# Loads of the next batch issued ahead of the peaks, and one subtraction given from GpSimd to VectorE

## The chip, the cores and the metric

One core of a Trainium2 chip runs the whole kernel. The time is the device time of one launch in microseconds (us), as the median of three timed runs. One more execution was profiled; its records are what the rows below show. The engines are named PE (TensorE), PEld (its weight loads), DVE (VectorE), ACT (ScalarE), POOL (GpSimd) and SP (SyncE, which only issues transfers here; its queue is SPq).

## What is computed

A transformer block on 32 sequences of 256 tokens with 128 features. The attention has 16 heads of 8 features. To the usual logits it adds an incidence of two lines per head, weighted by a decay to the power of the distance; behind it stand a gated residual and a top-2 mixture of 8 experts:

```python
logits = einsum('bhqd,bhkd->bhqk', q, k) * scale
write_lines = exterior(x_prev @ w1_write.T, x @ w2_write.T)     # six numbers per token and head
read_lines  = exterior(x @ w1_read.T, x @ w2_read.T)
incidence = einsum('bqhp,bkhp->bhqk', read_lines, write_lines @ J6)
bias = incidence * decays ** (q - k) * (q > k) * bias_scale
attn = softmax(where(q < k, -inf, logits + bias))
x = x + ga * (attn @ v @ w_out.T + b_out)
x = x + gb * sum over the two best experts of weight * FFN_e(layernorm(x) * (1 + cb) + sb)
```

## The kernel before

It has a setup, the attention part (`attend`, all that the change touches) and the experts' part. The attention part works batch by batch, one sequence of 256 tokens at a time, in iterations b = -4 to 35. Each iteration has eight slots, p = 0 to 7, one for each pair of heads, and each engine has its own list of work, written out slot by slot; an engine takes its list strictly in order and waits on semaphores in it. The lists are pipelined over batches: in iteration b the scores, exponentials and values of batch b are made, the prescores of batch b + 1 (from slot 1 on), the projections and lines of batches b + 2 and b + 3, and the end of batches b - 1 to b - 3.

Matrix products run in bf16. To keep the precision, each fp32 number is split in three bf16 parts: the high part (ACT copies, L1179), the rest (POOL subtracts, L1259), the middle part (ACT, L1182) and the low part (POOL subtracts once more, L1264, 96x768). The parts of the q and k features are `dim_part`, those of the lines `line_part`. Their place in the products is along the partitions, so they take a way through DRAM. SP stores `dim_part` to `dim_rows` (`store_dims`) and `line_part` to `line_rows` (`store_lines`), six transfers each (L649), and loads them from there:

- `load_rows` (L676, L677): rows of eight heads (a half) into `KT` and `QF` (`queries` in the rows): the dims' part from `dim_rows` and the decayed lines' part from `line_rows`, two transfers each. The prescores wait for these: half 0 in slot 1 of the iteration before, half 1 in slot 5.
- `load_lines` (L686): undecayed lines into `KI` and `QI`, for the incidences.
- `load_peaks` (L691): the prescores give each query's maximum (its peak), which DVE reduces (L919, L924), POOL splits in three parts, PE turns (jobs max0 and max1) and ACT copies to `peakT`; SP then loads it into three more rows of `QF`. The scores of the first slot wait for the peaks of half 0, those of the fifth slot (p = 4) for half 1.

SP's list is its `body`: it is in order too, so a transfer behind a wait comes no sooner than the wait's end. The waits are `hold(...)`: for `used["max0"]` and `used["max1"]` (the peaks are in `peakT`), `line_low` and `dim_low` (the low parts are made), `lines_stored` and `dims_stored` (stores have landed), `sc_ready`, `pre_ready` and `inc_ready` (the target's last readers are done).

On PE the names are `pre` (prescores, L759 to L761), `sc` (incidences L732, scores L745 to L748) and `bank` (the jobs). On DVE `weigh` multiplies `sc` by the decay (L950). On POOL `decayed` (L1367) opens an iteration, `outer_products` (L589, four products of 128x256) and `crosses` (L601, L603) make the lines of batch b + 3, `line_values` scales them, and L1360 scatters tokens to the experts.

## Time and profile before

| | us |
|---|---|
| median of three timed runs | 1115.75 |
| lowest, highest | 1115.15, 1118.87 |
| the profiled execution | 1110.27 |
| its span, first to last instruction | 1108.5 |
| busy in the span: PE, POOL, DVE, ACT | 921.3, 813.4, 788.8, 710.5 |

The profile has one row for a group of instructions or for one moment on one engine. In a row of a timeline the first number is the start in us from the span's start, the second how long it took, then the engine, the line of the kernel, the operation, what is written and read (names without their numbers), and the shapes. Brackets at the end give idle time of the engine just before it, and what ended it. "issue" there means that no cause shows. PE's matmuls overlap, so their times are not to be added.

### The profile page before, as it was taken

Reading aid. Unit: us, or ns where it says so; the run is one execution under the profiler, and the core shown is the slowest. Engines: PE = TensorE matmul, PEld = TensorE weight load, DVE = VectorE, ACT = ScalarE, POOL = GpSimd, SP = SyncE. Lnnn points to the kernel's source line nnn. Section 1 sums busy time; section 2 is a strip of 40 time slices with the busy share of each in tenths; the row PEclk is TensorE's granted clock in tenths of the full one; section 3 lists DMA queues with packets and bytes.
Section 4 is the critical chain, followed back from the end, with each engine's and each line's share of the span. In section 5 each row is a group of like instructions: output and inputs, shape, how many; then the busy total and the mean of one; then the engine's idle time right before and its main releaser. Section 6 shows DMA issues by size and latency. Waiting matters only on the chain. (4 is left out here: it accounts for less than half of the span.)

```text
span 1108.5 us, 30436 instructions
## 1 busy us (share of the span) xinstructions
PE 921.3 (83%) x9281; PEld 722.1 (65%) x9281; DVE 788.8 (71%) x2095; ACT 710.5 (64%) x1580; POOL 813.4 (73%) x1352
## 2 busy tenths in 40 slices
PE   2437989989988898898988888988862899999966
PEld 2325667767676666676766666766641788888852
DVE  7576768776788788787788878778756455566536
ACT  2345778777787777787777877777562455555520
POOL 8355678887888888888888888888345366666644
PEclk9999999998999999999999999999895899999989
DMA  7345565554565656656566565665411353333339
GB/s 189 114 127 150 160 163 145 155 160 139 153 173 148 176 148 161 168 144 179 145 165 164 151 176 141 161 167 152 119 50 48 84 167 88 95 92 92 86 140 349
DMA packets 233853, 160.37 MB, mean 145 GB/s; under 512 B 57376, under 2 KB 220512, under 8 KB 233568
## 3 DMA queue, kind: packets, MB, share of 16 engines
q1 hardware_dynamic: 222416, 133.77, 45.4%
q0 software_dynamic: 8448, 17.45, 5.1%
q10 hardware_dynamic: 2832, 7.20, 1.7%
q8 instruction: 81, 1.33, 0.6%
q14 instruction: 76, 0.62, 0.2%
HBM read 81.38 MB, written 76.19 MB: 142 GB/s over the span
## 5 line engine op out<-in xcount | busy, mean ns | idle before, releaser
L919 DVE TENSOR_REDUCE peak<-pre 128x6 f32<-128x768 f32 x256 | 244.2, 954 | 79.5 <-PE pre L761 76.5
L1152 ACT ACTIVATE PT<-sc 128x768 f32<-128x768 f32 x256 | 204.9, 800 | 31.0 <-PE sc L748 28.6
L950 DVE TENSOR_TENSOR sc<-sc,decay 128x512 f32<-128x512 f32 x256 | 177.2, 692 | 29.2 <-PE sc L732 25.5
L1638 POOL DMA_INDIRECT yab<-y_out,xt x136 | 131.6, 968 | 83.1 <-issue 63.3
L1360 POOL DMA_INDIRECT xg<-stage,slot_i x128 | 130.9, 1023 | 60.9 <-issue 31.2
L759 PE MATMUL pre<-KT,queries 84*128 84x128 bf16 x512 | 116.8, 228 | 58.6 <-DMA queries<-line_rows 52.3
L761 PE MATMUL pre<-causal,identb 128*128 128x256 bf16 x512 | 144.8, 283 | 0.0
L760 PE MATMUL pre<-KT,queries 84*128 84x256 bf16 x512 | 143.7, 281 | 0.0
L1592 DVE TENSOR_TENSOR hid<-silu,up 128x256 f32<-128x256 f32 x136 | 57.3, 421 | 82.6 <-ACT silu L1546 82.6
L745 PE MATMUL sc<-queries,KT 87*128 87x128 bf16 x512 | 101.8, 223 | 14.7 <-issue 3.6
L759 PEld LDWEIGHTS pre<-KT,queries 84*128 84x128 bf16 x512 | 51.2, 100 | 92.7 <-DMA queries<-line_rows 60.5
L1546 ACT ACTIVATE silu<-up 128x256 f32<-128x256 f32 x136 | 52.4, 385 | 88.9 <-PE up L1482 88.9
L732 PE MATMUL sc<-QI,KI 100*128 100x128 bf16 x1024 | 101.6, 222 | 0.0
L748 PE MATMUL sc<-queries,KT 87*128 87x128 bf16 x512 | 101.1, 222 | 0.0
L747 PE MATMUL sc<-queries,KT 87*128 87x128 bf16 x512 | 101.0, 222 | 0.0
L589 POOL TENSOR_TENSOR outer<-lines 128x256 f32<-128x256 f32 x116 | 80.7, 728 | 6.0 <-ACT lines L1117 6.0
L1498 PE MATMUL y<-w,hidT 128*128 x544 | 83.1, 275 | 0.1
L775 PE MATMUL pv<-PT,VP 128*32 128x256 f32 x1024 | 82.2, 393 | 0.0
L745 PEld LDWEIGHTS sc<-queries,KT 87*128 87x128 bf16 x512 | 50.9, 99 | 37.5 <-issue 25.9
L1498 PEld LDWEIGHTS y<-w,hidT 128*128 128x128 f32 x544 | 71.4, 191 | 0.3 <-issue 0.3
L732 PEld LDWEIGHTS sc<-QI,KI 100*128 100x128 bf16 x1024 | 70.3, 99 | 0.1
L1480 PE MATMUL up<-queries,x_hi 128*128 x136 | 66.0, 485 | 0.0
(275 smaller groups left out, 2672.1 us busy)
## 6 DMA issues: line engine op xcount, KB each, us to landing
line_rows<-line_part SPq DMA_DIRECT2D x64, 216.0 KB
dim_rows<-dim_part SPq DMA_DIRECT2D x64, 192.0 KB, 2.1
KT<-dim_rows SPq DMA_DIRECT2D x64, 192.0 KB
queries<-dim_rows SPq DMA_DIRECT2D x64, 192.0 KB
line_rows<-line_part SPq DMA_DIRECT2D x64, 144.0 KB
KI<-line_rows SPq DMA_DIRECT2D x64, 144.0 KB
QI<-line_rows SPq DMA_DIRECT2D x64, 144.0 KB
xt<-xg SPq DMA_DIRECT2D x136, 65.0 KB, 1.9
```

What stands on the lines that cost most here:

```text
L732: last = nc.tensor.matmul(seeded(p)[:, n, t, :], KI[0:INC, h, blk], QI[0:INC, h, blk], start=n == 0 and t == 0, stop=True, skip_group_chec ...
L745: nc.tensor.matmul(seeded(p)[:, n, 0, :], KT[par][0:TOP, h, first], QF[par][0:TOP, h, first], start=False, stop=True, skip_group_check=True)
L748: last = nc.tensor.matmul(seeded(p)[:, n, 1, :], KT[par][0:TOP, h, second], QF[par][0:TOP, h, second], start=False, stop=True, skip_group_ ...
L759: nc.tensor.matmul(pre[:, n, 0:P], QF[par][0:DIMS + LINES, h, 0:P], KT[par][0:DIMS + LINES, h, 0:P], start=True, stop=False)
L760: nc.tensor.matmul(pre[:, n, P:3 * P], QF[par][0:DIMS + LINES, h, P:T], KT[par][0:DIMS + LINES, h, :], start=False, stop=False)
L761: last = nc.tensor.matmul(diagonal(pre, n), identb[:], causal[:].unsqueeze(1).broadcast_to([P, 2, P]), start=False, stop=True)
L919: nc.vector.reduce_max(peak[half][:, i:i + 2, 0:3], pre[:, :, 0:3 * P].rearrange("p n (g k) -> p n g k", g=3), AX.X)\
L950: nc.vector.tensor_tensor(seeded(p), seeded(p), decay[:, 2 * p:2 * p + 2, :].unsqueeze(2).broadcast_to([P, 2, NT, P]), ALU.mult).then_inc( ...
L1152: nc.scalar.activation(PT[p % 4][:], sc[:, window], ACT.Exp).then_inc(exped.sem, 1)
L1360: nc.gpsimd.indirect_dma_start(xg[0:E * CAP, :], bass.IndirectOffsetOnAxis(slot_i[:, t, k:k + 1], 0), stage[par][:, t, k, :], None).then_i ...
L1498: last = nc.tensor.matmul(y[r % 2][:, 0:D], hidT[r % 2][:, m * P:(m + 1) * P], w3[:, span(e, 1), m, :].rearrange("p e d -> p (e d)"), star ...
L1638: nc.gpsimd.indirect_dma_start(yab, bass.IndirectOffsetOnAxis(xt[r][:, D:D + 1].bitcast(i32), 0), y_out[r % 8][:], None).then_inc(y_sent[r ...
```

## The change

`load_rows` is cut in two: `load_dims` loads the dims' part and `load_decayed` the lines' part. For half 1 both now stand at the head of SP's iteration, in front of the wait for the peaks of half 1. For half 0 the dims' part stands right behind the line stores, in front of the wait for the peaks of half 0, and the decayed part behind these peaks, in front of the lines of half 1. The low part of the lines (L1264) is taken from POOL's slot 3 and given to DVE's slot 3, behind that slot's reduce of the prescores.

```diff
-                def load_rows(jb, par, half):
+                def load_dims(jb, par, half):

                     hold(dims_stored, jb)
-                    hold(lines_stored, jb)
                     hold(sc_ready, jb - 2, 4 * half + 4)
                     hold(pre_ready, jb - 1, 4 * half + 1)
...
+                        sp.dma_start(tile[0:DIMS, heads, :], dim_rows[jb % 3][kq, :, heads, :]).then_inc(rows_loaded[half].sem, 16)
+
+                def load_decayed(jb, par, half):
+
+                    hold(lines_stored, jb)
+                    hold(sc_ready, jb - 2, 4 * half + 4)
...
+                        sp.dma_start(tile[DIMS:PEAK0, heads, kq * P:kq * P + P], line_rows[jb % 3][kq, :, heads, T:LW])\
+                          .then_inc(rows_loaded[half].sem, 16)
...
                 def body(b, par):
+                    if live(b + 1):
+                        load_dims(b + 1, 1 - par, 1)
+                        load_decayed(b + 1, 1 - par, 1)
                     if live(b):
                         load_peaks(b, par, 1)
                     if live(b + 1):
-                        load_rows(b + 1, 1 - par, 1)
                         load_lines(b + 1, 0)
                     if live(b + 2):
                         store_lines(b + 2)
+                        load_dims(b + 2, par, 0)
                     if live(b + 1):
                         load_peaks(b + 1, 1 - par, 0)
+                    if live(b + 2):
+                        load_decayed(b + 2, par, 0)
+                    if live(b + 1):
                         load_lines(b + 1, 1)
-                    if live(b + 2):
-                        load_rows(b + 2, par, 0)
                     if live(b + 3):
                         store_dims(b + 3)
```

The subtraction:

```diff
+                    if p == 3 and live(b + 2):
+                        wait(dve, line_mid, b + 2)
+                        nc.vector.tensor_tensor(line_part[:, 2, :], line_rest[:], line_part[:, 1, :], ALU.subtract).then_inc(line_low.sem, 1)
...
-                        if p == 3 and live(b + 2):
-                            wait(pool, line_mid, b + 2)
-                            nc.gpsimd.tensor_tensor(line_part[:, 2, :], line_rest[:], line_part[:, 1, :], ALU.subtract).then_inc(line_low.sem, 1)
```

How the lists stand in one iteration. SP before, from the peaks of half 0 (first row) over the lines and the rows to the six stores of the dims:

```order
98 L691 DMA queries<-peakT 3x8x256
99 L686 DMA KI<-line_rows 36x8x256
100 L686 DMA QI<-line_rows 36x8x256
101 L676 DMA KT<-dim_rows 48x2048
102 L677 DMA KT<-line_rows 36x8x128
103 L676 DMA queries<-dim_rows 48x2048
104 L677 DMA queries<-line_rows 36x8x128
105 L649 DMA dim_rows<-dim_part 128x3x256
```

SP now, from the end of the line stores to the first store of the dims:

```order
97 L649 DMA line_rows<-line_part 96x384
98 L675 DMA KT<-dim_rows 48x2048
99 L675 DMA queries<-dim_rows 48x2048
100 L697 DMA queries<-peakT 3x8x256
101 L683 DMA KT<-line_rows 36x8x128
102 L683 DMA queries<-line_rows 36x8x128
103 L692 DMA KI<-line_rows 36x8x256
104 L692 DMA QI<-line_rows 36x8x256
105 L649 DMA dim_rows<-dim_part 128x3x256
```

The dims' loads moved in front of the peaks, and the decayed loads in front of the lines. Next comes the head of the following iteration. SP before, from the last store of the dims:

```order
110 L649 DMA dim_rows<-dim_part 128x256
111 L691 DMA queries<-peakT 3x8x256
112 L676 DMA KT<-dim_rows 48x2048
113 L677 DMA KT<-line_rows 36x8x128
114 L676 DMA queries<-dim_rows 48x2048
115 L677 DMA queries<-line_rows 36x8x128
116 L686 DMA KI<-line_rows 36x8x256
```

SP now, at the same place:

```order
110 L649 DMA dim_rows<-dim_part 128x256
111 L675 DMA KT<-dim_rows 48x2048
112 L675 DMA queries<-dim_rows 48x2048
113 L683 DMA KT<-line_rows 36x8x128
114 L683 DMA queries<-line_rows 36x8x128
115 L697 DMA queries<-peakT 3x8x256
116 L692 DMA KI<-line_rows 36x8x256
```

All four loads of half 1 now stand between the stores and the peaks of half 1. POOL before, from the rest (L1259) to the counts of the experts:

```order
474 L1259 TENSOR_TENSOR line_rest<-line_val,line_part 96x768
475 L589 TENSOR_TENSOR outer<-lines 128x256 x4
476 L1264 TENSOR_TENSOR line_part<-line_rest,line_part 96x768
477 L601 TENSOR_TENSOR cross<-outer 128x2x2x48
478 L603 TENSOR_TENSOR cross<-outer 128x4x16 x3
```

DVE now, around its fourth slot, where L929 is the reduce of the prescores and L960 the multiply by the decay:

```order
595 L960 TENSOR_TENSOR sc<-sc,decay 128x512
596 L929 TENSOR_REDUCE peak<-pre 128x2x3
597 L991 TENSOR_TENSOR line_part<-line_rest,line_part 96x768
598 L1017 TENSOR_REDUCE slot_i<-slot_pick 128x4
599 L1021 TENSOR_SCALAR eg<-egap 128x2
600 L1023 RECIPROCAL stage<-eg 128x2
601 L1026 TENSOR_SCALAR stage<-egap,stage 128x1 x2
602 L960 TENSOR_TENSOR sc<-sc,decay 128x512
```

The row L1264 is gone from POOL, so `crosses` follows `outer` directly, and it is L991 on DVE.

## Rows read from the trace of the kernel before

**Rows 1.** Stretches: us, busy of PE, PEld, DVE, ACT, POOL, clock, DMA, GB/s

```profile
93.90:203.80 109.90, 98.48 (x1162) 75.84 (x1162) 80.68 (x171) 82.30 (x157) 82.07 (x154) 1.00 0.58 156
203.80:302.80 99.00, 88.06 (x983) 69.28 (x982) 71.50 (x178) 71.94 (x144) 81.74 (x150) 0.91 0.54 149
302.80:762.60 459.80, 410.96 (x4901) 317.68 (x4900) 372.83 (x881) 361.29 (x720) 402.64 (x740) 0.99 0.60 160
762.60:821.60 59.00, 49.20 (x612) 36.95 (x612) 43.41 (x115) 35.59 (x64) 26.57 (x58) 0.94 0.44 114
234.50:237.90 3.40, 3.40 (x19) 3.34 (x18) 1.22 (x2) 0.60 (x1) 2.12 (x4) 0.50 0.22 64
```

**Rows 2.** Timeline of POOL over one regular batch

```profile
397.80 0.72 POOL L1367 TENSOR_TENSOR line_val<-line_val,line_decay 96x256 f32<-96x256 f32 x1
...
399.13 0.20 POOL L1331 CAST peak_part<-peak_rest 128x16 bf16<-128x16 f32 x1 [0.17 <-POOL peak_rest L1328]
...
402.90 2.78 POOL L589 TENSOR_TENSOR outer<-lines 128x256 f32<-128x256 f32 x4
405.64 1.66 POOL L1264 TENSOR_TENSOR line_part<-line_rest,line_part 96x768 bf16<-96x768 f32 x1
407.25 0.60 POOL L601 TENSOR_TENSOR cross<-outer 128x192 f32<-128x192 f32 x1
...
419.65 1.16 POOL L1293 TENSOR_TENSOR dim_part<-dim_rest,dim_part 128x512 bf16<-128x512 f32 x1
420.76 0.73 POOL L1367 TENSOR_TENSOR line_val<-line_val,line_decay 96x256 f32<-96x256 f32 x1
```

**Rows 3.** Timeline of PE: scores of the fifth slot, prescores of the second

```profile
405.75 0.22 PE L745 MATMUL sc<-queries,KT 87*128 87x128 bf16 x1 [0.23 <-issue]
...
421.56 0.23 PE L759 MATMUL pre<-KT,queries 84*128 84x128 bf16 x1 [1.38 <-DMA queries<-line_rows]
```

**Rows 4.** Timeline of SP in the same batch

```profile
402.62 0.76 SPq L691 DMA_DIRECT2D queries<-peakT  x1
...
407.90 2.89 SPq L649 DMA_DIRECT2D line_rows<-line_part  x6
414.14 0.74 SPq L691 DMA_DIRECT2D queries<-peakT  x1
...
416.16 0.32 SPq L676 DMA_DIRECT2D KT<-dim_rows  x1
...
420.91 3.04 SPq L649 DMA_DIRECT2D dim_rows<-dim_part  x6
```

**Rows 5.** Waits of PE, first and last stretch: total us, times, longest

```profile
PE pre L759 <- DMA queries<-line_rows: 9.4, 9, 1.9
...
PE pre L759 <- DMA queries<-line_rows: 4.2, 2, 2.3
```

**Rows 6.** Timeline of PE before a stretch at half clock

```profile
233.92 0.23 PE L759 MATMUL pre<-KT,queries 84*128 84x128 bf16 x1 [2.35 <-DMA queries<-line_rows]
```

**Rows 7.** DVE with two inputs from SBUF, and POOL beside it

```profile
L589 DVE TENSOR_TENSOR outer<-lines 128x256 f32<-128x256 f32 x12 | 4.3, 421 | 10.5 <-ACT lines L1117 10.5
...
419.84 1.03 DVE L970 TENSOR_TENSOR hot<-iota,topi 128x32 f32<-128x32 f32 x1
...
1098.78 0.68 DVE L1624 TENSOR_TENSOR ya<-ya,x_all 128x512 f32<-128x512 f32 x1
...
1098.95 1.64 POOL L1645 TENSOR_TENSOR ya<-ya,x_all 128x512 f32<-128x512 f32 x1 [0.46 <-DVE ya L1617]
```

**Rows 8.** Timeline of DVE around the subtraction's new place

```profile
403.90 0.96 DVE L919 TENSOR_REDUCE peak<-pre 128x6 f32<-128x768 f32 x1
...
406.51 0.70 DVE L950 TENSOR_TENSOR sc<-sc,decay 128x512 f32<-128x512 f32 x1 [0.23 <-PE sc L732]
407.96 0.96 DVE L919 TENSOR_REDUCE peak<-pre 128x6 f32<-128x768 f32 x1 [0.75 <-PE pre L761]
```

**Rows 9.** Timeline of ACT at the middle part of the lines

```profile
402.97 0.84 ACT L1182 ACTIVATE line_part<-line_rest 96x768 bf16<-96x768 f32 x1 [0.44 <-POOL line_rest L1259]
```

More of the change, by code:

```diff
@@ L666, in store_lines @@
                         spread(slots(line_rows[jb % 3][kq]), line_part[:, :, kq * LW:(kq + 1) * LW], kq, lines_stored.sem)
-                def load_rows(jb, par, half):
+                def load_dims(jb, par, half):
                     hold(dims_stored, jb)
+                    hold(sc_ready, jb - 2, 4 * half + 4)
+                    hold(pre_ready, jb - 1, 4 * half + 1)
+                    heads = slice(8 * half, 8 * half + 8)
+                    for kq, tile in ((0, KT[par]), (1, QF[par])):
+                        sp.dma_start(tile[0:DIMS, heads, :], dim_rows[jb % 3][kq, :, heads, :]).then_inc(rows_loaded[half].sem, 16)
+                def load_decayed(jb, par, half):
                     hold(lines_stored, jb)
                     hold(sc_ready, jb - 2, 4 * half + 4)
-                    hold(pre_ready, jb - 1, 4 * half + 1)
-                    heads, done = slice(8 * half, 8 * half + 8), rows_loaded[half].sem
+                    heads = slice(8 * half, 8 * half + 8)
                     for kq, tile in ((0, KT[par]), (1, QF[par])):
-                        sp.dma_start(tile[0:DIMS, heads, :], dim_rows[jb % 3][kq, :, heads, :]).then_inc(done, 16)
-                        sp.dma_start(tile[DIMS:DIMS + LINES, heads, kq * P:kq * P + P],
-                                     line_rows[jb % 3][kq, :, heads, T:LW]).then_inc(done, 16)
+                        sp.dma_start(tile[DIMS:PEAK0, heads, kq * P:kq * P + P], line_rows[jb % 3][kq, :, heads, T:LW])\
+                          .then_inc(rows_loaded[half].sem, 16)
                 def load_lines(jb, half):
```

## Prediction

> **What bounds the kernel now.** I started with the stretches of the span [rows 1]. The attention part, 94 to 822 us, is the only part that the change touches. Between 302.80 and 762.60, 20 batches take 459.80 us, 22.99 each. PE is busy 410.96 us of that and POOL 402.64, so the shares do not say which of them is the limit. The order of time does. On POOL [rows 2] the decay multiply (L1367) opens one batch at 397.80 and the next at 420.76: 22.96 us. Read the starts and ends of the rows between: each begins where the one before ends, and where the row carries a wait it is a wait for POOL's own result (0.17 us). POOL is a chain with no slack, and most batches of this stretch repeat its 22.96 to within 0.03. So here the batch lasts as long as POOL's list of work.
>
> PE meanwhile has one halt per batch that it would not have by its own work [rows 3]: the prescores of the second slot start at 421.56 after 1.38 us of waiting for the rows of half 0. SP shows why [rows 4]: the peaks of half 0 are issued at 414.14, then the lines, and only at 416.16 the rows, which land 5.4 us later, at 421.56. Without the halt PE would need 22.96 - 1.38 = 21.58 us a batch. POOL is the longer of the two, so in the regular stretch the halt is idle time of an engine that is not the limit.
>
> It is the limit elsewhere. In the first stretch, 93.90 to 203.80, the rows cost PE 9.4 us in nine halts, and in the last, from 762.60, 4.2 us in two [rows 5]; POOL is busy only 82.07 of 109.90 us and 26.57 of 59.00 us there [rows 1]. Between 203.80 and 302.80 four batches take 24.75 us each and the granted clock is 0.91. The halt that ends at 233.92 lasted 2.35 us [rows 6], and from 234.50 to 237.90 the clock is 0.50, the 1.2 GHz level [rows 1]. I read it so: a long halt of PE comes first, then a stretch at half clock, and that one delays the next rows again.
>
> **The change part by part.** *The last subtraction leaves POOL.* L1264 starts at 405.64 and the next row at 407.25 [rows 2]: 1.61 us off POOL's chain. What stands behind it is `crosses`, which waits for `outer`, POOL's own result. Until now 1.61 us of other work lay between them. A wait for an own result costs 0.17 us where it shows in [rows 2], and nothing at all if the result is ready; I take 0.12 back.
>
> *It comes to VectorE.* The trace has no 96x768 subtraction on VectorE. Two inputs from SBUF at 256 columns take 0.42 us (L589, alone), at 512 columns 0.68 (L1624) [rows 7]: 0.26 more for 256 more, so 0.94 us for 768. Its place is behind the reduce that starts at 403.90 and ends at 404.86 [rows 8]. Its input is there: ACT's middle part runs 402.97 to 403.81 [rows 9]. VectorE has 0.75 us of waiting for PE in front of the reduce at 407.96 [rows 8], plus 0.23 in front of the multiply at 406.51; 0.98 us covers 0.94. What is over (waiting for a port, below) delays the multiply by some 0.3 to 0.7 us, and its reader, the scores of the sixth slot, has PE's own prescores in front of it. So I cost VectorE at nothing in the regular stretch.
>
> *But it holds POOL up.* This is where I chose. In the last part of the kernel POOL adds 128x512 from SBUF while VectorE does an addition with both inputs in SBUF: VectorE's runs from 1098.78 to 1099.46, POOL's starts at 1098.95 and takes 1.64 us [rows 7]. POOL's own subtraction of 128x512 takes 1.16 (419.65) [rows 2]; the 0.48 more is just the time to VectorE's end. It goes the other way too: L970, a comparison of 128x32, takes 1.03 us and ends at 420.87, 0.06 after POOL's subtraction ends at 420.81 [rows 7, 2]. The new subtraction would start at 404.86, while POOL is in its four `outer` products (402.90 to 405.68) [rows 2]. It waits out the product that runs, up to 0.7 us (2.78 / 4), and then holds the next for its own 0.94. Bounds: 0 (the products don't mind) and 0.94; I take 0.94, because the rows show both directions.
>
> The Trainium skill (SBUF — State Buffer, SBUF: two separate sides) says that VectorE with two SBUF inputs and a GpSimd instruction that reads SBUF share one pair of ports, and that whoever is second is blocked for the whole instruction; the trace agrees (0.48 and 1.03 us). It speaks against this change. The same skill (GPSIMD Engine Reference, Engine selection) sends elementwise work to VectorE as about twice as fast, which by itself would make the move worth its full 1.61 us, 30 us in this stretch instead of 11.
>
> POOL's chain is then 22.96 - 1.61 + 0.12 + 0.94 = 22.41 us, still above PE's 21.58. The 20 batches gain 20 x 0.55 = **11.0 us**.
>
> *Rows of half 1 in front of the peaks of half 1.* They were issued behind the peaks (402.62). Now they follow the six stores of the dims, which end at 420.91 + 3.04 = 423.95 [rows 4], so they are out by about 426, and need to be there by the prescores of the sixth slot, some 6 us later. These halts go. The price is on the peaks, which now stand behind four big loads (rivals).
>
> *Rows of half 0.* The dims' part goes in front of the peaks' wait, right behind the line stores. These end at 407.90 + 2.89 = 410.79 today; on SP nothing happens until 414.14, so this part is free. With VectorE's result at about 405.9 in place of 407.30 the stores themselves start up to 1.4 us earlier. The decayed part follows the peaks at about 415.2, ahead of the lines. PE is due at 421.56 - 1.38 = 420.18. With today's 5.4 us from the first issue to the last landing the decayed part is there at 420.6, 0.4 late; but it is two loads and not four, and the lines' loads stand behind it and not in front. So of the halt 0 to 0.4 us is left; I take 0.
>
> *What the halts give.* 203.80 to 302.80: without long halts the clock should stay up, and POOL's chain is next: 4 x (24.75 - 22.41) = 9.4 us; I take **8**, since one fall may stay. 93.90 to 203.80: of 9.4 us I take **5.5**, as the last batches there meet POOL's 22.41. From 762.60: **3.5** of 4.2.
>
> Sum: 11.0 + 8 + 5.5 + 3.5 = 28 us. The profiled execution took 1110.27 us (span 1108.5), so 1082.3. The median of the three timed runs is 1115.75, 5.5 above it; I carry the difference along: **1088 us**, 2.5% faster. Its own range is 1080 to 1095.
>
> **Rivals.**
> *POOL is not held.* Then its chain is 21.47 and PE's 21.58 is next: 20 x 1.38 = 27.6, 12.7 in the four batches, 7 and 4 outside: 51 us, 1065. For it: L589 on VectorE ran at 0.42 us in the prologue, which shows that nothing is lost when POOL is not reading at the time; a product of 0.7 us may leave gaps between its reads. Against: [rows 7].
> *The halt moves to the peaks of half 1.* They are issued behind the rows, which follow the stores of the dims: rows out from about 424.2, landing 4.6 to 5.4 us later (5.4 as above; the lower end is an estimate, since the lines are not in front), 428.8 to 429.6, and the peaks just behind. PE's scores of the fifth slot, at 405.75 now [rows 3], are due at 428.71: a wait of 0.1 to 0.9 us in the regular stretch. There it costs little, since PE has 22.41 - 21.58 = 0.83 us to spare, and it cannot be earlier by itself: the exponential in front of it stands behind ACT's middle part, which waits for POOL (0.44 us) [rows 9]. In the other stretches, where PE leads, it could eat most of the 17 us: 1115.75 - 11 - 3 = 1101 (1095 to 1107). The same result comes if the decayed rows of half 0 still come late.
> *Slower.* The same mechanism, larger. If the peaks land more than 0.83 us after PE is due, the batch is PE's: 21.58 + w. From w = 1.38 (landing about 1.4 us behind PE's own due time) it is longer than now. At w = 2, with the peaks behind six stores and four loads, it is 0.6 us a batch, 17 us over 28 batches, and halts of this size are those that the half clock followed: 3.4 us at 0.50 costs 1.7 us of PE. That gives 1133, and 1120 with few falls. Against it: the loads start as soon as dims are stored, and 28 batches would all have to lose.
> *No change.* POOL's hold grows to what was taken off (a wait for an own result of 0.17, a second product held) and the clock falls stay.
>
> **How the numbers follow.** Forecast 0.52 (1088); POOL not held 0.13 (1065); moved halt 0.20 (1101); no change 0.07; slower 0.08 (1133). Faster by over 0.3% (3.3 us, about what a measurement of this kernel can tell): 0.85; within: 0.07; slower: 0.08. The range leaves out the far half of the first rival and all of the last two: 1066 to 1107.
>
> **What the new profile would show.** Right: L1264's work on VectorE at 0.95 to 1.65 us, one `outer` product per batch at about 1.65 in place of 0.73, POOL without waits and a period of 22.4 us; the rows' waits in front of the prescores nearly gone; the clock near 1.00 between 204 and 303 us. POOL unheld: `outer` at 0.73 throughout and a period of 21.5. Moved halt: PE waits at the scores for `queries<-peakT`. Most likely to make me wrong is the hold: its size is from one pair of operations in another part of the kernel.

## The result, and the profile after

The changed kernel took **1104.05 us** (median of 4 runs, 1099.33 to 1107.09), beside 1117.31 us for the kernel before (median of 4, 1115.15 to 1121.72). The ratio is 0.9877, with a 95% interval of 0.9837 to 0.9918: 13 us or 1.2% faster. The forecast was 1088 us, a gain of 28. The sign held, and the time lies in the wide range of 1066 to 1107, but outside the forecast's own of 1080 to 1095. A little less than half of the gain came, and the time is near that of the rival "the halt moves to the peaks of half 1" (1101).

The profiled execution took 1104.48 us, its span 1102.7. That is 0.4 us above its own median, while the profiled execution of before lay 7 us below its median; so the two traces show only 5.8 us of the 13. The stretches of after run between the same places as those of [rows 1] (start of the scores of batches 0, 5, 9 and 29, end of the last scores). The columns are the stretch and its length, busy time of PE, PEld, DVE, ACT and POOL, the granted clock, DMA share and GB/s:

```profile
94.00:203.50 109.50, 99.91 (x1163) 76.47 (x1164) 86.20 (x176) 82.98 (x157) 78.69 (x150) 0.95 0.61 158
203.50:294.60 91.10, 81.88 (x982) 63.74 (x982) 77.28 (x181) 73.03 (x144) 77.56 (x145) 0.98 0.63 162
294.60:762.60 468.00, 415.50 (x4902) 322.00 (x4902) 383.08 (x902) 365.51 (x720) 385.22 (x721) 0.96 0.60 157
762.60:816.90 54.30, 46.25 (x612) 35.21 (x611) 43.44 (x117) 35.64 (x64) 24.15 (x56) 1.00 0.43 116
```

Against [rows 1] the first stretch gains 0.4 us (5.5 expected), the second 7.9 (8), the last 4.7 (3.5). The twenty regular batches, which were to gain 11.0, **lose 8.2**: 23.40 us each instead of 22.99. POOL's busy time there fell as meant, from 402.64 to 385.22 us. The clock fell too, from 0.99 to 0.96.

PE's waits over the whole span tell which thing came last now (total us, times, longest):

```profile
PE sc L755 <- DMA queries<-peakT: 57.3, 32, 3.9
...
PE pre L769 <- DMA queries<-line_rows: 2.5, 1, 2.5
```

L755 is the scores' first product (L745 before) and L769 the prescores' (L759 before). The rows' waits of [rows 5] and of the regular stretch ([rows 3]: 1.38 us) are gone but for one. In their place stand 57.3 us of waiting for peaks: one wait in every batch from 1 to 30 at the fifth slot, for the peaks of half 1, and two of 0.5 us for those of half 0.

How that comes about is seen in a bad batch, 452.8 to 479.4. POOL first, and the same list in time order for SP, ACT and PE:

```profile
455.20 1.16 POOL L1303 TENSOR_TENSOR dim_part<-dim_rest,dim_part 128x512 bf16<-128x512 f32 x1
...
472.73 0.20 POOL L1336 CAST peak_part<-peak 128x16 bf16<-128x16 f32 x1 [4.13 <-DVE peak L934]
```

```profile
456.45 3.52 SPq L649 DMA_DIRECT2D dim_rows<-dim_part  x6
460.23 0.99 SPq L675 DMA_DIRECT2D KT<-dim_rows  x1
461.27 0.42 SPq L675 DMA_DIRECT2D queries<-dim_rows  x1
461.87 0.31 SPq L683 DMA_DIRECT2D KT<-line_rows  x1
462.23 0.41 SPq L683 DMA_DIRECT2D queries<-line_rows  x1
462.76 0.74 SPq L697 DMA_DIRECT2D queries<-peakT  x1
```

```profile
460.27 0.37 ACT L1138 ACTIVATE peakT<-bank 24x256 bf16<-24x256 f32 x1 [0.18 <-PE bank L828]
```

```profile
467.48 0.27 PE L755 MATMUL sc<-queries,KT 87*128 87x128 bf16 x1 [3.85 <-DMA queries<-peakT]
```

ACT has the peaks ready at 460.64. SP issues their load at 462.76, 2.12 us later, since it has first to issue the six stores of the dims (from 456.45, right behind POOL's low part, 456.36) and four loads. (The loads need the dims stored one iteration earlier, so it is the order of SP's list that ties them to these stores, and not their landing.) From the issue to PE's start it is another 4.72 us. PE's late scores make its prescores late, DVE's maxima with them, and POOL then waits 4.13 us for DVE. POOL's low part of the next dims comes out of the same list, and the next peaks stand behind it. The change tied PE's fifth slot to POOL by way of SP, and so made a ring: POOL's dims, stores, loads of rows, load of peaks, scores, prescores, maxima, POOL.

A plain batch (203.5 to 225.7, 22.21 us) has the same order with less of it:

```profile
206.78 3.04 SPq L649 DMA_DIRECT2D dim_rows<-dim_part  x6
210.09 0.33 SPq L675 DMA_DIRECT2D KT<-dim_rows  x1
...
211.96 0.75 SPq L697 DMA_DIRECT2D queries<-peakT  x1
```

```profile
215.53 0.22 PE L755 MATMUL sc<-queries,KT 87*128 87x128 bf16 x1 [1.56 <-DMA queries<-peakT]
```

Of the 24 batches between 203.5 and 762.6, sixteen have a halt of 0.95 to 1.92 us there and eight one of 2.3 to 3.9. The batches with a halt of up to about 1.6 us and a full clock last 21.6 to 22.3, as if there were none. The eight last 24.0 to 26.6. The second thing that they have, most of them, is the clock. These are stretches of after again: the bad batch, one without a fall, and the fall in the bad one:

```profile
452.80:479.40 26.60, 22.37 (x246) 16.93 (x245) 18.82 (x46) 18.44 (x36) 19.60 (x37) 0.87 0.51 139
524.70:546.80 22.10, 20.05 (x246) 15.61 (x246) 19.33 (x46) 18.15 (x36) 19.23 (x37) 1.00 0.59 165
...
465.70:472.50 6.80, 5.02 (x37) 3.47 (x38) 1.80 (x4) 2.58 (x5) 2.14 (x6) 0.50 0.73 219
```

The halt starts at 463.63, the clock goes to 0.50 (1.2 GHz) at 465.7, within it, and is back at 472.5. PE is busy 2.3 us longer in that batch for the same 246 products.

The last part of the change that the trace shows is the hold of POOL. DVE's subtraction (L991) and POOL beside it, in another regular batch, and the group of the products on the page (busy us, mean ns of one):

```profile
394.95 1.42 DVE L991 TENSOR_TENSOR line_part<-line_rest,line_part 96x768 bf16<-96x768 f32 x1
```

```profile
393.47 3.49 POOL L589 TENSOR_TENSOR outer<-lines 128x256 f32<-128x256 f32 x4
397.03 0.59 POOL L601 TENSOR_TENSOR cross<-outer 128x192 f32<-128x192 f32 x1
```

```profile
L589 POOL TENSOR_TENSOR outer<-lines 128x256 f32<-128x256 f32 x116 | 99.9, 892 | 1.0 <-ACT lines L1130 1.0
```

The four products took 2.78 us [rows 2] and take 3.49 now: 0.71 more, all of it in one of the four (27 of the 116 products take 1.43 to 1.45 us, the others some 0.73).

### The profile page after: what moved, and what is told of

The parts are those of the page before. It is cut to its first block and busy times, and to the rows that moved or that the text cites. A ratio compares the mean times of both kernels' runs of the same rounds, so it can differ in the third digit from the quotient of the medians.

```text
span 1102.7 us, 30500 instructions
## 1 busy us (share of the span) xinstructions
PE 917.4 (83%) x9281; PEld 719.1 (65%) x9281; DVE 812.4 (74%) x2127; ACT 716.0 (65%) x1580; POOL 782.5 (71%) x1320
## 3 DMA queue, kind: packets, MB, share of 16 engines
q8 instruction: 81, 1.33, 0.5%
## 5 line engine op out<-in xcount | busy, mean ns | idle before, releaser
L929 DVE TENSOR_REDUCE peak<-pre 128x6 f32<-128x768 f32 x256 | 243.9, 953 | 56.5 <-PE pre L771 53.6
L960 DVE TENSOR_TENSOR sc<-sc,decay 128x512 f32<-128x512 f32 x256 | 177.0, 692 | 46.8 <-PE sc L742 41.4
L755 PE MATMUL sc<-queries,KT 87*128 87x128 bf16 x512 | 101.8, 224 | 64.9 <-DMA queries<-peakT 57.3
L769 PE MATMUL pre<-KT,queries 84*128 84x128 bf16 x512 | 116.9, 228 | 9.8 <-DVE peak L929 6.3
L1602 DVE TENSOR_TENSOR hid<-silu,up 128x256 f32<-128x256 f32 x136 | 57.3, 421 | 81.3 <-ACT silu L1556 81.3
L755 PEld LDWEIGHTS sc<-queries,KT 87*128 87x128 bf16 x512 | 51.4, 100 | 92.3 <-issue 76.7
L589 POOL TENSOR_TENSOR outer<-lines 128x256 f32<-128x256 f32 x116 | 99.9, 892 | 1.0 <-ACT lines L1130 1.0
L769 PEld LDWEIGHTS pre<-KT,queries 84*128 84x128 bf16 x512 | 51.5, 101 | 38.3 <-issue 15.3
```

The lines of the kernel that those rows point to most:

```text
L755: nc.tensor.matmul(seeded(p)[:, n, 0, :], KT[par][0:TOP, h, first], QF[par][0:TOP, h, first], start=False, stop=True, skip_group_check=True)
L769: nc.tensor.matmul(pre[:, n, 0:P], QF[par][0:DIMS + LINES, h, 0:P], KT[par][0:DIMS + LINES, h, 0:P], start=True, stop=False)
L929: nc.vector.reduce_max(peak[half][:, i:i + 2, 0:3], pre[:, :, 0:3 * P].rearrange("p n (g k) -> p n g k", g=3), AX.X)\
L960: nc.vector.tensor_tensor(seeded(p), seeded(p), decay[:, 2 * p:2 * p + 2, :].unsqueeze(2).broadcast_to([P, 2, NT, P]), ALU.mult).then_inc( ...
```

## The experiments

Each run is compared with runs of the kernel before on the same chip. "Middle" is the length of batches 5 to 28, from the trace, over 24. There is one trace for each kernel.

| kernel | median us | ratio to before (95%) | middle us per batch |
|---|---|---|---|
| before | 1115 to 1118 | 1 | 23.28 |
| after | 1104.05 | 0.9877 (0.9837 to 0.9918) | 23.30 |
| e1: after, rows of half 1 back | 1079.31 | 0.9681 (0.9635 to 0.9727) | 22.20 |
| e2: new order, subtraction on POOL | 1114.95 | 0.9998 (0.997 to 1.0026) | 23.39 |
| e3: before, subtraction on DVE | 1105.73 | 0.9902 (0.9858 to 0.9947) | 22.92 |
| e4: before, rows of half 0 moved | 1101.91 | 0.9857 (0.981 to 0.9904) | 22.96 |
| e5: after, peaks of half 1 on ACT's queue | 1081.23 | 0.9717 (0.9664 to 0.977) | 22.21 |
| e8: after, only the dims' rows in front | 1087.54 | 0.972 (0.967 to 0.977) | 22.82 |
| e6: e1, subtraction one slot later | 1132.33 | 1.0125 (1.0077 to 1.0173) | 23.84 |
| e9: e1, subtraction of 32 columns | 1062.09 | 0.9517 (0.9467 to 0.9566) | 21.52 |
| e10: e1, two steps of POOL on ACT | 1058.02 | 0.9477 (0.9426 to 0.9528) | 21.37 |

My theory after the result: the rows of half 1 in front of the peaks cost what is missing, by the ring above. The rivals: the subtraction on DVE does harm (by the hold, or by making DVE late), or the new order of half 0 does.

### e1: the rows of half 1 behind the peaks again

```diff
                 def body(b, par):
-                    if live(b + 1):
-                        load_dims(b + 1, 1 - par, 1)
-                        load_decayed(b + 1, 1 - par, 1)
                     if live(b):
                         load_peaks(b, par, 1)
                     if live(b + 1):
+                        load_dims(b + 1, 1 - par, 1)
+                        load_decayed(b + 1, 1 - par, 1)
                         load_lines(b + 1, 0)
```

> The changed kernel with one thing put back: the four row loads of half 1 stand behind the peaks of half 1 again. Half 0 in two parts and the subtraction on VectorE stay. Theory A (the peaks of half 1 land late because they stand behind the row loads of half 1): PE's 57 us of waiting for the peaks at the fifth slot go to near 0, the prescores' waits stay under 10 us, the regular batch takes what POOL's chain takes, 22.96 - 1.61 + 0.71 + 0.1 = 22.2 us, and the time is 25 to 32 us under the kernel before. Theory B (the peaks are late because the whole stream of transfers is too dense since the subtraction and half 0 came earlier): most of the 57 us stays, and the time is within 5 us of the changed kernel.

It took 1079.31 us (1077.91 to 1081.23), 3.2% under the kernel before (1116.12). That is theory A, with a larger gain than its 25 to 32 us (36.8). The stretch of batches 5 to 28, PE's waits (whole span) and POOL's (in that stretch) in this kernel:

```profile
203.30:736.20 532.90, 491.25 (x5882) 375.24 (x5881) 464.34 (x1082) 432.10 (x864) 463.04 (x865) 1.00 0.63 166
```

```profile
PE pre L768 <- DMA queries<-line_rows: 8.2, 10, 2.3
...
PE sc L754 <- DMA queries<-peakT: 4.9, 9, 0.9
```

```profile
POOL xg L1369 <- issue: 29.4, 84, 0.7
```

and POOL's in the same batches of after (203.5 to 762.6):

```profile
POOL peak_part L1336 <- DVE peak L934: 26.3, 19, 4.1
```

Two things follow. The 559.1 us of after are 26.2 more than the 532.9 here, and after's POOL waits 26.3 us for DVE's maxima, which here it does not wait for at all. The loss of the middle batches is the ring. And the waits for rows are 8.2 us in ten, not the 52.3 in 41 of before. All ten are of half 1, and the kernel before had such waits too. Two of before's, both at the sixth slot and so for half 1, then one of e1's:

```profile
109.42 0.23 PE L759 MATMUL pre<-KT,queries 84*128 84x128 bf16 x1 [1.04 <-DMA queries<-line_rows]
152.53 0.23 PE L759 MATMUL pre<-KT,queries 84*128 84x128 bf16 x1 [1.04 <-DMA queries<-line_rows]
```

```profile
109.88 0.23 PE L768 MATMUL pre<-KT,queries 84*128 84x128 bf16 x1 [1.47 <-DMA queries<-line_rows]
```

Sorted by slot, before's 9.4 us in the first stretch are 6.1 us of half 0 and 3.3 us of half 1; in batches 5 to 28 they are 35.0 us of half 0 and 1.6 us of half 1. So **in the middle batches the rows of half 1 had hardly ever been late**, and there the move of half 1 paid for nothing. In the first batches they had been, and were again in e1 (4.4 us from 94.1 to 203.3). The clock is 1.00 over the middle stretch of e1.

### e2 and e3: each part of the change by itself

e2 puts the subtraction back on POOL and keeps the new order.

```diff
-                    if p == 3 and live(b + 2):
-                        wait(dve, line_mid, b + 2)
-                        nc.vector.tensor_tensor(line_part[:, 2, :], line_rest[:], line_part[:, 1, :], ALU.subtract).then_inc(line_low.sem, 1)
...
+                        if p == 3 and live(b + 2):
+                            wait(pool, line_mid, b + 2)
+                            nc.gpsimd.tensor_tensor(line_part[:, 2, :], line_rest[:], line_part[:, 1, :], ALU.subtract).then_inc(line_low.sem, 1)
```

> The whole new order of SP, with the subtraction back on POOL. If POOL's chain is what binds the regular batch, as I read it, its period is again 22.96 us or more, and the wait for the peaks of half 1 shows here too (0.1 to 0.9 us a batch by the landing estimate). Time: 0 to 8 us under the kernel before. If POOL's list was no limit, this kernel is as fast as the changed one, 13 us under before.

1114.95 us (10 runs, 1109.96 to 1117.75), ratio 0.9998: the new order alone is worth nothing. Its waits for peaks are nearly those of after, and POOL's products are at their old length:

```profile
PE sc L755 <- DMA queries<-peakT: 51.9, 31, 3.6
```

```profile
L589 POOL TENSOR_TENSOR outer<-lines 128x256 f32<-128x256 f32 x116 | 80.7, 725 | 1.1 <-ACT lines L1127 1.1
```

So the halt at the peaks is not made by DVE's subtraction, and the hold is.

e3 is the kernel before with the subtraction on DVE and the old order; against the kernel before, its edit is the subtraction's part of the change and nothing else.

> The kernel before with the subtraction on VectorE and nothing else. POOL's chain is then 22.2 us, but PE's halt for the rows of half 0 stays in the loop. In stretches where POOL caught up before, the batch took 22.2 to 22.6 us with this halt. So the regular batch takes 22.3 to 22.8 us; gain 4 to 12 us. If the halt alone had bound the batch, the gain is 0; if POOL alone had, it is 15 us or more.

1105.73 us (10 runs, 1100.08 to 1115.6), 10 us faster. Here PE halts for the rows as before, 41.7 us in batches 5 to 28 (before: 36.5), and the clock in those batches is 0.97. It is less the halts than the clock that lengthens them: 9 of the 24 have a fall of the clock and last 23.8 to 26.0 us, the other 15 have halts of 1.2 to 2.6 us and a median length of 22.1. The kernel before has seven batches with a fall. The group of L601 in e3:

```profile
L601 POOL TENSOR_TENSOR cross<-outer 128x192 f32<-128x192 f32 x29 | 24.5, 845 | 2.3
```

POOL's four products are at 724 ns here, but this one is at 845 instead of 601 (and L603 at 385 instead of 326). So in e3 DVE's subtraction meets another instruction of POOL, or none.

### e4: the rows of half 0 moved, and nothing else

The diff to after is that of e1 and that of e2 together.

> The kernel before with the new order of half 0 alone: half 1 stays behind its peaks and the subtraction on POOL. PE's waits for the rows go to near 0 and so do the stretches at half clock; the regular batch stays at POOL's 22.96 us. The gain is what the other stretches give, 12 to 20 us. If the halts had been the limit in the regular batch too, the period falls below 22.9 and the gain comes near the 36 us of the kernel with the subtraction on VectorE.

1101.91 us (1099.49 to 1104.22) beside 1118.13. Nearly all the rows' waits are gone, with half 1 in its old place; nine of the ten left are of half 1:

```profile
PE pre L768 <- DMA queries<-line_rows: 6.9, 10, 2.3
...
PE sc L754 <- DMA queries<-peakT: 2.3, 5, 0.7
```

The middle batches last 22.96 us, as POOL's chain in [rows 2], and the clock over them is 1.00, with one fall in 24 batches. That is the prediction's reading of what bounds the kernel, seen from the other side: with the halts of half 0 gone and POOL's list untouched, the batches at full clock do not get shorter, and the 7.8 us that the middle gains are those of the batches with a fall.

These four and the two whole kernels make a table of parts. The subtraction alone gives 10 us, half 0 alone 16, both 37 (e1): each takes away what limits the other. By the ratios, half 1 costs some 16 us on top of e4 (e2: 0.9998 against 0.9857) and some 22 on top of e1 (after: 0.9877 against 0.9681).

### e5: the peaks of half 1 loaded from ACT's queue

What in the order makes the halt: that the peaks' load is issued late, or that it travels behind the rows? In e5 the order of SP is that of after, but ACT issues the load of these peaks itself, right behind its copy.

```diff
-                    if live(b):
-                        load_peaks(b, par, 1)
...
                                 evacuate(name, jb, jb % 2)
+                                if name == "max1":
+                                    wait(act, used["max1"], jb)
+                                    act.dma_start(QF[jb % 2][PEAK0:TOP, 8:16, :], peakT[1][:]).then_inc(peak_loaded[1].sem, 16)
```

> The changed kernel with the peaks of half 1 loaded from ACT's own DMA queue, right behind ACT's copy, in place of SP's. The row loads of half 1 stay at the head of SP's iteration. If the peaks were late because they stood in SP's list and in SP's queue behind the rows, they land about 2.3 us after issue and the 57 us of waits go below 10; the time is 22 to 32 us under before, less up to 0.8 us a batch that the issue may cost ACT. If the 16 DMA engines' bandwidth is what makes them late, they land 3.4 us or more after issue and at least half of the waits stays.

1081.23 us (1079.43 to 1086.13), 35 us under before and nearly as e1. ACT's copy, its load, and PE's start in one batch, and PE's waits over the span:

```profile
211.59 0.37 ACT L1136 ACTIVATE peakT<-bank 24x256 bf16<-24x256 f32 x1 [0.18 <-PE bank L826]
212.00 0.74 ACTq L1189 DMA_DIRECT2D queries<-peakT  x1
```

```profile
215.64 0.22 PE L753 MATMUL sc<-queries,KT 87*128 87x128 bf16 x1 [0.69 <-DMA queries<-peakT]
```

```profile
PE sc L753 <- DMA queries<-peakT: 23.5, 24, 2.0
```

The load is out 0.04 us after the copy, and it is still 3.64 us until PE starts. In after's plain batch it was 3.57. Over all middle batches in which PE waited for these peaks, the time from issue to PE's start is 3.64 to 4.45 us in e5 (median 3.90) and 2.39 to 4.72 in after (median 3.65). In the kernel before, where a load of peaks with no rows just ahead of it is seen to release PE, it is issued at 781.92 and PE starts at 784.29, 2.37 us. And in e10 below, where the same peaks go out 0.5 to 2.0 us behind the six stores but in front of the rows, PE starts 2.83 us after the issue without any wait in 22 of 24 middle batches, so they had landed by then. So both of the expectation's cases are half true. With the rows' loads beside it the small load mostly takes some 1.2 us longer, **whichever queue it is in** (in this batch of e5 two of the four loads go out just before it and two just after); and on SP's queue it is issued later besides, 1.33 us after the copy (median of the middle batches in after). One pause stays unexplained: in e1 PE stands still for 0.62 us at this place in nearly every batch, up to 3.51 us after the issue, and the profile names no cause. For the time only the later issue matters. In the middle batches, 16 waits of up to 1.5 us, 14.9 in all, leave them at 22.21 us, as 5 waits for peaks and 2.7 us do in e1. POOL, which sets those, does not wait for DVE's maxima here. In these kernels a halt of PE below some 1.6 us is free; it is the longer ones that turn the ring.

### e8: only the dims' rows in front of the peaks

```diff
                     if live(b + 1):
                         load_dims(b + 1, 1 - par, 1)
-                        load_decayed(b + 1, 1 - par, 1)
                     if live(b):
                         load_peaks(b, par, 1)
                     if live(b + 1):
+                        load_decayed(b + 1, 1 - par, 1)
```

> The changed kernel with only two of the four row loads of half 1 (the dims' part, 384 of 528 KB) in front of its peaks, the decayed part behind them. If the peaks wait for what stands in front of them, they are issued 0.8 us earlier and land up to 0.7 us sooner after issue: PE's 57 us of waiting falls to 15 to 35, and the time is between the changed kernel and the one with nothing in front, 20 to 30 us under before. If the kind of load in front makes no difference, it stays at the changed kernel's 13 us.

1087.54 us (1082.29 to 1090.13). Two loads in front of the peaks instead of four, and between the two ends: PE waits 27.5 us for peaks (22 times, longest 2.4). The loads of peaks do not land sooner after their issue than in after (median 3.61 us until PE starts, against 3.65, where the expectation had up to 0.7 less); they are issued sooner, 0.43 us after the copy (median) and not 1.33. POOL's wait for the maxima in batches 5 to 28 is

```profile
POOL peak_part L1336 <- DVE peak L934: 14.9, 10, 2.6
```

The stretch (199.4 to 747.0) is 547.6 us long, 14.7 more than e1's: again the length of that one wait. What PE waits in total does not give the price; POOL's wait does.

e8 also shows what moving half 1 can buy. Its first stretch takes 105.3 us (94.1 to 199.4), where the kernel before takes 109.9 and e1 109.2: the rows' halts of half 1 are gone there, and no halt at the peaks has come in their place.

### e6: the subtraction one slot later

The hold comes from DVE's subtraction falling on POOL's products. In the next slot POOL scatters, and the products are over; so I moved it there, from e1.

```diff
-                    if p == 3 and live(b + 2):
+                    if p == 4 and live(b + 2):
```

> The fastest kernel so far (half 1 behind its peaks, half 0 in two parts, subtraction on VectorE) with VectorE's subtraction one slot later, in its fifth. There POOL has its wait of 0.7 us and a scatter. If the hold needs a POOL instruction that reads SBUF, all four outer products take 0.73 us again and POOL's chain is 21.5 us. But the line stores start some 3 us later, and the decayed rows and the peaks of half 0 stand behind them: either PE waits for those up to 1 us a batch. Between 15 us faster than that kernel (only the hold counts) and 10 us slower (only the late stores count); I expect 5 slower.

1132.33 us (1128.47 to 1136.53), 1.25% **slower** than before, and by the ratios 4.6% slower than e1, for one digit. That is about 50 us, where I expected 5. The products are free (DVE 0.94 us, POOL's products 726 ns), but the hold is not all gone: DVE's subtraction now overlaps a short copy of POOL's, 0.20 us alone:

```profile
298.55 0.63 POOL L1335 CAST peak_part<-peak 128x16 bf16<-128x16 f32 x1
```

The larger loss is elsewhere. The line stores wait for this subtraction. SP, ACT and PE at the next first slot, and POOL's wait in batches 5 to 28:

```profile
415.49 2.86 SPq L649 DMA_DIRECT2D line_rows<-line_part  x6
418.61 0.31 SPq L675 DMA_DIRECT2D KT<-dim_rows  x1
418.97 0.42 SPq L675 DMA_DIRECT2D queries<-dim_rows  x1
419.80 0.73 SPq L697 DMA_DIRECT2D queries<-peakT  x1
```

```profile
419.33 0.37 ACT L1137 ACTIVATE peakT<-bank 24x256 bf16<-24x256 f32 x1 [0.17 <-PE bank L827]
```

```profile
423.52 0.22 PE L754 MATMUL sc<-queries,KT 87*128 87x128 bf16 x1 [1.29 <-DMA queries<-peakT]
```

```profile
POOL peak_part L1335 <- DVE peak L933: 37.0, 25, 4.2
...
POOL dim_part L1302 <- ACT dim_part L1220: 10.3, 5, 2.4
```

The peaks of half 0 are issued 0.10 us after their copy, so nothing stands in their way on SP; but the six stores and the two loads of dims have just gone out, and PE starts 3.72 us after the issue. It is the effect of e5, at the other half: what is in flight counts, not only what is in front in SP's list. The account of the middle batches needs more than the wait for the maxima this time: against e9 below, which has no hold, they are 55.7 us longer, 37.0 for the maxima, 10.3 for ACT's middle part of the dims, and 8.4 in which POOL is busy, which is about what that copy takes longer.

### e9: what the hold is worth

e9 is e1 with DVE's subtraction on 32 of the 768 columns. The low parts of the other columns are left out; a memset before the batches, not shown, makes them zero.

```diff
-                        nc.vector.tensor_tensor(line_part[:, 2, :], line_rest[:], line_part[:, 1, :], ALU.subtract).then_inc(line_low.sem, 1)
+                        nc.vector.tensor_tensor(line_part[:, 2, 0:32], line_rest[:, 0:32], line_part[:, 1, 0:32], ALU.subtract).then_inc(line_low.sem, 1)
```

> The fastest kernel so far with VectorE's subtraction on 32 of the 768 columns; the low part of the other columns is left out (zero). VectorE's instruction falls from 0.95 us to about 0.2, so nothing of POOL is held for longer than 0.1 us. If the hold and POOL's chain bound the batch, its period falls from 22.2 to 21.5 or 21.6 us (21.58 is PE's own), and 12 to 17 us of time go. If PE or ACT bind already, it stays at 22.2 and the time within 3 us.

1062.09 us (1061.03 to 1063.51), 4.8% under the kernel before where e1 is 3.2% under it. The instruction itself, still at the same place (duration ns, least, median and most), and its neighbour on POOL:

```profile
L990 DVE TENSOR_TENSOR line_part<-line_rest,line_part x32: 178/660/675, 59.8 to 729.4; 96x32 bf16<-96x32 f32 x32
```

```profile
L589 POOL TENSOR_TENSOR outer<-lines 128x256 f32<-128x256 f32 x116 | 80.7, 727 | 1.1 <-ACT lines L1130 1.1
```

The instruction takes 0.18 us alone and 0.66 beside POOL: it waits 0.48 us for a product of POOL to end, which with 0.95 + 0.48 is also the 1.42 of the full one. Its own 0.18 us hold nobody. The middle batch is 21.52 us, 0.68 under e1's 22.20, close to the 0.71 of the hold, and POOL's chain is still what the batch follows.

### e10: two small steps of POOL on ACT

If POOL's chain is the limit in e1, anything taken off it counts, where ACT has room (432.10 of 532.90 us busy). The two 128x2 steps of the second norm (L1321, L1322 in after) go to ACT's first slot. Nothing of the computation is left out.

```diff
+                        if p == 0 and live(b - 2):
+                            wait(act, var2, b - 2)
+                            wait(act, shift2, b - 3)
+                            nc.scalar.activation(ve2[:], mv2[:, :, 1], ACT.Copy, bias=EPS).then_inc(norm_step2.sem, 1)
+                            nc.scalar.activation(nm2[:], mv2[:, :, 0], ACT.Copy, scale=-1.0).then_inc(norm_step2.sem, 1)
...
-                    wait(pool, var, jb)
-                    settle(pool, pool_settled)
-                    nc.gpsimd.tensor_scalar(ve[:], mv[:, :, 1], EPS, None, ALU.add).then_inc(stepped.sem, 1)
-                    nc.gpsimd.tensor_scalar(nm[:], mv[:, :, 0], -1.0, None, ALU.mult).then_inc(stepped.sem, 1)
```

> The fastest kernel so far with two more short instructions taken from POOL: the two steps of the second norm (128x2, 0.31 us each from start to start) are done by ACT in the slot before. POOL's chain is 22.2 - 0.6 = 21.6 us; ACT, busy 18 us a batch, gets 0.5 us more. If POOL's list binds the batch: 12 to 15 us faster than that kernel, 48 to 52 us under before. If ACT's new work delays the exponentials, or PE binds: within 4 us of it.

**1058.02 us** (1055.62 to 1059.71), 5.2% under the kernel before (1115.14), 57 us where I expected 48 to 52, and the fastest of all; it beats both kernels of this study. The middle batch went from 22.20 to 21.37, 0.83 us, for 0.62 us of instructions. POOL and DVE in one batch:

```profile
404.26 2.79 POOL L589 TENSOR_TENSOR outer<-lines 128x256 f32<-128x256 f32 x4
407.13 1.20 POOL L601 TENSOR_TENSOR cross<-outer 128x192 f32<-128x192 f32 x1
```

```profile
406.51 1.36 DVE L990 TENSOR_TENSOR line_part<-line_rest,line_part 96x768 bf16<-96x768 f32 x1
```

The hold has moved: POOL is ahead by those 0.6 us, its products end in peace, and DVE's subtraction now falls on L601, which takes 1.20 us instead of 0.60. It waits 0.41 us for the last product, runs its own 0.95 and ends at 407.87; POOL's instruction ends 0.46 later. The hold is 0.6 instead of 0.71, which is part of the 0.83. PE's waits for rows are up again (16.7 us, 16 times), all of them for half 1: as the batch gets shorter, the old place of half 1 begins to be late in the middle batches too (8.3 us there). PE is close behind POOL by now.

## Why the prediction was right, and where it failed

**What bounds the kernel: right.** POOL's list sets the regular batch; e4 (22.96 with PE's halts gone) and e9 and e10 (each shortening of POOL arrives at the end) show it. The reading of the rows was a little too clean. Between the rows of [rows 2] POOL has other pauses than those for its own results, in front of its four scatters:

```profile
409.80 1.10 POOL L1360 DMA_INDIRECT xg<-stage,slot_i  x1 [0.69 <-DVE peak L924]
```

Over the 24 middle batches they add up to nearly the same in before, after, e1, e6, e9 and e10 (32.7 to 33.8 us), so I count them as part of the list's length.

**POOL's chain: right.** It was to be 22.96 - 1.61 + 0.12 + 0.94 = 22.41 us. In e1, where nothing else stands in the way, it is 22.20. The hold was the term chosen between 0 and 0.94; it measured 0.71, so its mechanism was right and its size 0.23 us too large. The rest, 0.14, agrees with the 0.12 for the own result. The place was right too: one of the four products. The rival "POOL is not held" gets its number from e9: without the hold it would have been 0.7 us a batch more, some 16 us over the middle batches.

By the Trainium skill (SBUF — State Buffer, SBUF: two separate sides) whoever of the two comes second at the shared pair of ports is blocked for the whole instruction of the other. The traces agree but for 0.14 us: POOL's product in after ends 0.59 us after DVE's subtraction where alone it takes 0.73, and e10's L601 ends 0.46 after it where alone it takes 0.60. With a start just behind DVE's, that is why the hold is 0.71 and not 0.95. The Trainium skill (GPSIMD Engine Reference, Engine selection) sends elementwise work to VectorE as about twice as fast as GpSimd. Here it is 0.95 us against 1.65, and the 0.71 of the hold comes back from it.

**The rows of half 0: right.** I left nothing of the halt, and in after, e1 and e4 no prescores of batches 5 to 28 wait for rows of half 0 (35.0 us before). The 1.9 and 1.4 us of such waits that e1 and e4 have there are of half 1.

**DVE at no cost: right.** DVE's work is 1.42 us, within 0.95 to 1.65, and in e1, which has it too, the middle batches' waits for DVE add up to 0.2 us at PE and 2.9 at POOL.

**203.8 to 302.8: right** (8 forecast, 7.9 in after, 10.0 in e1). **The first stretch: wrong**, of 5.5 us came 0.4 in after and 0.7 in e1. The traces show what stood there: in after, where the rows' halts are gone, 4.8 us of waiting for the peaks and one fall of the clock (192.6), in e1 4.4 us of rows of half 1 and one fall (132.1). e8 has neither, no fall and 105.3 us, a gain of 4.6. So the term had a right size and came out only where neither half was late. The stretch varies between kernels up to 119.1 us (e6), and with one trace each I can't say how much of that is chance.

**The rows of half 1: here the prediction failed**, in three steps. In its sum the peaks that wait behind these rows cost nothing; by the traces of after and e1 they cost some 23 us.

*Little was bought.* I wrote "These halts go" of half 1, and no row stood behind it. [rows 3] shows a halt at half 0, [rows 5] adds up the line without saying which half. Of the 52.3 us before, 46.0 are of half 0; half 1 has 1.6 us in the middle batches and 3.3 in the first stretch. e4, with half 1 in its old place, has 6.9 us left over the whole span. A look at which slot the waits are in would have said so.

*The price was mis-sized.* I put the wait for the peaks at 0.1 to 0.9 us, from a landing at 428.8 to 429.6. It was 0.95 to 3.94 in the regular batches, 1.8 on average over the 32 waits. In a plain batch the landing was nearly right: from the end of the six stores to PE's start it is 5.71 us (209.82 to 215.53), which from the forecast's 423.95 gives 429.7. Against the 428.71 at which PE was to be due that is a wait of 0.95, and it was 1.56. So most of the error there is PE: I took its own batch as 21.58, the period less the halt. But some of PE's other waits of the batch before were slack as well; in e10 the middle batches last 21.37 on average and the shortest 20.84. So PE arrives earlier than I thought and waits longer, and, for the same reason, can afford more: not 0.83 us but some 1.6.

*"It costs little" was true of most batches and not of eight.* In those the halt was 2.3 to 3.9 us, POOL had to wait for PE's maxima, and most were followed by a stretch at half clock. Their share is what turned a gain into a loss in the middle: the eight halts are some 12 us over 1.6 each, and nine batches with a fall of the clock have PE busy 1.3 to 2.7 us longer. The sum, an estimate of some 27 us, is close to the 26.2 that e1 does not have. The "slower" rival had this mechanism (ring and clock) and its threshold of w about 1.4; I thought that "28 batches would all have to lose", but eight were enough to take back what sixteen gained.

What stays open is why it was those eight. In all of them the peaks were issued late, 1.64 to 2.80 us after ACT's copy (most of the others: about 1 us), and PE started 3.2 to 4.7 us after the issue; four others had an issue 1.5 to 2.2 us late too, but there PE started 2.4 to 2.8 us after it. In five of the eight the six stores took 3.5 to 4.9 us to issue instead of 3.04 (3.52 in the bad batch above), in the other three the loads of rows came more slowly. Why SP was slower just there no run was made to tell.

With e1's number the forecast reads as follows: the parts that were argued from rows give 29.0 us in the profiled executions (1110.27 to 1081.23), for 28 forecast, and the one part that had no row took about 23 back. That the 29.0 meets the 28 is in part luck. The profiled execution of before is a fast one, and by the medians e1 gains 36.8 us. And by stretches e1 gains 0.7, 10.0, 15.9 and 1.9 us, where 5.5, 8, 11.0 and 3.5 were forecast: the errors of the first and the third cancel.

## What to carry to other kernels

A transfer in front of another in a queue is a price on the one behind, even when SP has time: look first whether the one moved forward had ever been waited for, by slot and not by line. A small load that an engine waits for should go out before the big ones whose readers come later. And where an engine has spare time per batch, a halt costs nothing up to that, and beyond it everything: price halts by the wait that they cause at the engine that sets the period (here POOL's for the maxima, 0, 14.9 and 26.3 us in e1, e8 and after, against 0, 14.7 and 26.2 us of time). That price is of one wait only: in e6, with 37.0 us of it, other waits and a hold come to another 19 us against e9.

## What the runs showed of the hardware

- The load of `peakT` (24x256) took 2.37 us from issue to the start of its reader with no loads of rows just ahead, 3.57 behind four of them on the same queue (2.39 to 4.72 over the middle batches, median 3.65), and 3.64 on another engine's queue with two of the four just ahead and two just behind (3.64 to 4.45, median 3.90). Another queue gave an earlier issue, not a faster landing. Behind six stores and two loads that had just been issued (e6) it was 3.72. Two loads ahead and not four (e8) left it at a median of 3.61.
- DVE's subtraction, with two inputs in SBUF, and POOL's instructions beside it exclude each other nearly whole, and the collision moves: on the fourth product in after and e1, on the next instruction in e10, on a 0.20 us copy in e6, sometimes on none in e3. The subtraction's place in DVE's list is the same in all of these but e6. In most batches DVE waits up to some 0.5 us for its turn. POOL's product takes 0.71 us longer, L601 up to 0.80 (e3).
- The granted clock fell to 0.50 inside a halt (from 463.63; fall at 465.7), not only after it. But it did not fall in every batch with a long halt: the one of 3.10 us in batch 12 (361.1 to 385.2) passed at 1.00, and one of 1.83 us in batch 14 was followed by a fall. e1 and e5, whose halts are below 1.5 us in the middle, have 1.00 there. What decides it was not tried.
